# The routed mixtures of layers 0 and 2 run in two halves of eight batches instead of one pass over sixteen

## The chip, the cores and the metric

One core of a Trainium2 chip runs the whole kernel. The metric is device time in microseconds, from one launch, as the median of several executions. One execution was also recorded by the profiler, and all rows below are from it. TensorE is PE in the rows (PEld its weight loads), VectorE is DVE, ScalarE ACT, GpSimd POOL, and SyncE, which only issues DMAs here, SP.

## The reference, cut to what matters

A tower of four layers works on x, 16 batches of 128 tokens of width 128. Each layer adds a gated cross attention and a gated feed-forward part to x. The feed-forward parts of layers 0 and 2 are mixtures of eight experts. The reference lets each token's two best experts count (layer 2 shown):

```python
    logits = jnp.einsum('btd,de->bte', x, Wg) + bg
    top2_vals, top2_idx = jax.lax.top_k(logits, 2)
    scores = jax.nn.softmax(top2_vals, axis=-1)
    onehot = jax.nn.one_hot(top2_idx, E, dtype=x.dtype)
    combine = jnp.einsum('btk,btke->bte', scores, onehot)
    h = jnp.einsum('btd,edh->bteh', x, W1) + b1[None, None]
    h = jax.nn.gelu(h, approximate=False)
    y = jnp.einsum('bteh,ehd->bted', h, W2) + b2[None, None]
    out = jnp.einsum('bted,bte->btd', y, combine)
    return _layer_norm(x + out, gamma, beta)
```

Layer 0 has two first matrices (silu of one times the other), a threshold in place of the product as such, and no outer normalisation. Layer 1's feed-forward part is a chain of four dense matrices (Mlp in the kernel), layer 3's a third mixture that isn't routed by lists.

## The kernel before, in words

The program is a row of phases: Attn0, Routed0, Mlp, Attn2, Routed2, Attn3, Experts3. Each engine has its own instruction list, written out by hand. At the end of a phase, `end_phase` (L163) lets four engines drain and all wait for each other.

**Router, beside the attention.** Batches are taken in four groups of four. While the attention runs, `Router` (L1023) finishes what it can for each group, in phases of one attention step: statistics and normalised x (XNB, stored to the tensor xn in memory), its turn, logits, first and second maximum (`dve_first`, `dve_second`), sums over tokens, ranks (`ranked`), places, and lists. A list says which token stands at which row of which expert. It is made on TensorE by a product of two one-hot sets, AT (128x128, VectorE) and BT (128x128, POOL), eight each. Group g can start only when its four batches leave the attention. So the last groups' phases remain when the attention is over: `tail` (L1174) runs six more steps (TAIL = 6) on every engine with nothing beside them. In it also come `pe_tiles` and `pe_tokens` (L1153, L1164), which turn counts and lists into the table: the expert of each tile, its tokens (IDX) and first rows.

**Tiles.** 4096 pairs of token and expert fill tiles of 128 rows, each of one expert. Each expert may end in a part-filled tile, so 32 + 7 = 39 tiles are run, whatever the routing (NT, L1630). `Routed` is a software pipeline over them: POOL gathers a tile's rows of x (XG, L1696, three tiles ahead) and makes ONE (L1705), a one-hot set that picks the expert's bias row; TensorE turns XG (L1727); ScalarE and VectorE split the result in two parts, XH and XL (L1734, L1739); TensorE makes the products with three pairs of parts and the bias (L1756 to L1759). In step i TensorE does the turn of tile i+1, the first products of i, the turn of the hidden values of i-1 and the second product of i-2 (`pe`, L1761). In layer 0 ScalarE makes SG, VectorE TT (L1910) and, behind the turn, ST (L1924); in layer 2 ScalarE makes SG and SH, VectorE SL (L1988). Y is then taken out by VectorE and stored by SP to the tensor ys. The weights of a tile are chosen by a register with the expert's number, read from the table.

The turned hidden values alternate between two PSUM banks in layer 0 (`pe_units`, L1912). Its second weights W2 are cast in this phase: two of four 1024-column pieces are loaded by SP at its start to a buffer of their own.

**Sums.** For each batch POOL gathers two rows of ys per token (GA, L2197), and VectorE adds both with their weights (L2204, L2207). This is done in the next phase: in Mlp (L2405, L2466) batches 0 to 3 come before anything else, the others between; in Attn3 (`dve_sum`, L2740) batch by batch. ys is written until the end of the tiles, so no gather can begin earlier.

## Time and profile before

| | |
|---|---|
| median of 3 runs | 1191.19 us (1189.45 to 1194.58) |
| the profiled execution | 1195.1 us, its span 1193.8 us |
| TensorE busy, share of span | 907.6 us, 76% |
| VectorE busy | 663.1 us, 56% |
| POOL busy | 474.8 us, 40% |
| ScalarE busy | 396.4 us, 33% |
| mean granted clock of TensorE | 0.833 |
| chain that ended last | TensorE 57%, VectorE 19%, issue 8%, POOL 7%, DMA 5% |

The busy times say how long an engine worked, not whether something waited for it. The stages differ: some are one full engine, others a chain of short steps over many engines. The granted clock is the share of full speed at which TensorE was allowed to run; 1.0 is 2.4 GHz and 0.5 is 1.2 GHz. The kernel is read by stages, and a stage by its timeline.

### The profile page before, as it was taken

Reading aid. Unit: us, or ns where it says so; the run is one execution under the profiler, and the core shown is the slowest. Engines: PE = TensorE matmul, PEld = TensorE weight load, DVE = VectorE, ACT = ScalarE, POOL = GpSimd, SP = SyncE. Lnnn points to the kernel's source line nnn. Section 1 sums busy time; section 2 is a strip of 40 time slices with the busy share of each in tenths; the row PEclk is TensorE's granted clock in tenths of the full one; section 3 lists DMA queues with packets and bytes.
Section 4 is the critical chain, followed back from the end, with each engine's and each line's share of the span. In section 5 each row is a group of like instructions: output and inputs, shape, how many; then the busy total and the mean of one; then the engine's idle time right before and its main releaser. Section 6 shows DMA issues by size and latency. Waiting matters only on the chain.

```text
span 1193.8 us, 22685 instructions
## 1 busy us (share of the span) xinstructions
PE 907.6 (76%) x8131; PEld 723.2 (61%) x8131; DVE 663.1 (56%) x1792; ACT 396.4 (33%) x737; POOL 474.8 (40%) x786
## 2 busy tenths in 40 slices
PE   3776675299992698896777763899658888888898
PEld 2455464278881577675566553799536666777555
DVE  3677663566664655542356544455565676641565
ACT  0343341032221232331244320455402445543412
POOL 5443433444434455225455444555273444200100
PEclk9988665589996699998699855899855999986999
DMA  5211111111123100001122200221211000000262
GB/s 180 82 48 54 33 32 45 66 30 45 45 39 94 47 18 14 5 1 43 54 55 64 59 10 9 56 54 51 47 43 43 26 23 26 16 8 10 63 203 89
DMA packets 48843, 57.59 MB, mean 48 GB/s; under 512 B 7008, under 2 KB 34688, under 8 KB 48352
## 3 DMA queue, kind: packets, MB, share of 16 engines
q1 hardware_dynamic: 43760, 45.65, 12.7%
q0 software_dynamic: 4544, 9.32, 3.3%
q8 instruction: 70, 1.15, 0.4%
q10 hardware_dynamic: 432, 1.18, 0.2%
q14 instruction: 37, 0.30, 0.1%
HBM read 42.02 MB, written 8.32 MB: 42 GB/s over the span
## 4 chain that ended last, share of the span: by engine, by line
PE 57%; DVE 19%; issue 8%; POOL 7%; DMA 5%; ACT 3%; SPq 1%; POOLq 0%; DVEq 0%; ACTq 0%
PE banks L412 9%; DVE NM L482 6%; PE banks L420 4%; PE bank L181 4%; PE bank L433 3%; PE banks L175 3%; PE banks L177 3%; PE banks L176 3%; PE banks L1756 3%; PE bank L2108 2%; POOL BT L1377 2%; PE banks L1759 2%; PE banks L1758 2%; PE banks L1757 2%; PE bank L1999 2%
## 5 line engine op out<-in xcount | busy, mean ns | idle before, releaser
L412 PE MATMUL banks<-KT,QT 31*128 31x128 f32 (+1 forms) x1280 | 165.1, 395 | 95.6 <-DVE NM L482 49.0
L482 DVE TENSOR_REDUCE NM<-banks 128x4 f32<-128x1024 f32 (+1 forms) x112 | 136.6, 1219 | 127.6 <-PE banks L412 127.4
L412 PEld LDWEIGHTS banks<-KT,QT 31*128 31x128 f32 x1280 | 116.4, 230 | 129.5 <-DVE NM L482 56.7
L456 ACT ACTIVATE EE<-banks 128x1024 f32<-128x1024 f32 x112 | 114.7, 1024 | 202.0 <-PE banks L420 201.9
L420 PE MATMUL banks<-QT,KT 32*128 32x128 f32 x1792 | 164.3, 329 | 3.5 <-ACT EE L456 2.5
L420 PEld LDWEIGHTS banks<-QT,KT 32*128 32x128 f32 x1792 | 136.1, 225 | 8.6 <-issue 7.5
L1696 POOL DMA_INDIRECT XG<-xn,SL x78 | 80.2, 1028 | 21.6 <-issue 12.8
L2197 POOL DMA_INDIRECT GA<-ys,PI x64 | 68.1, 1064 | 40.9 <-DMA ys<-Y 25.3
L433 PE MATMUL bank<-EE,VV 128*32 128x128 f32 x1792 | 78.0, 325 | 0.8 <-ACT EE L456 0.8
L1705 POOL TENSOR_SCALAR ONE<-CP,EC 128x128 fp32r<-128x128 f32 x78 | 30.4, 389 | 95.2 <-PE bank L1938 54.9
L433 PEld LDWEIGHTS bank<-EE,VV 128*32 128x32 f32 x1792 | 56.2, 129 | 13.3 <-issue 9.2
L175 PE MATMUL banks<-HH,W1H 128*128 128x512 f32 x128 | 52.5, 411 | 8.2 <-DVE HH L2464 8.1
L1734 ACT CAST XH<-bank 128x128 fp32r<-128x128 f32 x78 | 20.7, 266 | 109.7 <-PE bank L1727 109.7
L1377 POOL TENSOR_SCALAR BT<-CP,PR 128x128 fp32r<-128x128 f32 x64 | 45.9, 733 | 19.1 <-DVE PR L1279 19.1
L177 PE MATMUL banks<-HH,W1L 128*128 128x512 f32 x128 | 51.3, 401 | 0.0
L1988 DVE TENSOR_TENSOR SUL<-bank,SUH 128x512 fp32r<-128x512 f32 x39 | 27.0, 692 | 43.3 <-ACT SUH L1983 43.3
L176 PE MATMUL banks<-HH,W1H 128*128 128x512 f32 x128 | 51.0, 398 | 0.0
L2464 DVE TENSOR_TENSOR HH<-GG,HH 128x512 fp32r<-128x512 f32 x32 | 23.3, 739 | 46.8 <-POOL HH L2485 46.8
L1924 DVE TENSOR_SCALAR ST<-bank 128x512 fp32r<-128x512 f32 x39 | 27.0, 691 | 38.7 <-PE bank L181 38.7
L1759 PE MATMUL banks<-BI,ONE 128*128 128x512 f32 x117 | 47.2, 403 | 0.0
L1999 PE MATMUL bank<-W,SUH 128*128 x156 | 41.3, 342 | 1.4 <-DVE Y L1827 1.4
L2370 ACT ACTIVATE GG<-banks,VC 128x512 f32<-128x512 f32 x32 | 21.6, 687 | 49.5 <-PE banks L177 47.4
(369 smaller groups left out, 2331.3 us busy)
## 6 DMA issues: line engine op xcount, KB each, us to landing
RAW<-in_w SPq DMA_DIRECT2D x20, 512.0 KB, 3.8
CBS<-cw SPq DMA_DIRECT2D x32, 256.0 KB, 3.6
ys<-Y SPq DMA_DIRECT2D x78, 64.0 KB, 1.5
RAW<-in_w SPq DMA_DIRECT2D x8, 352.0 KB, 3.3
KT<-in_keys SPq DMA_DIRECT2D x8, 256.0 KB, 3.1
KT<-KQ SPq DMA_DIRECT2D x32, 64.0 KB, 1.9
QT<-KQ SPq DMA_DIRECT2D x32, 64.0 KB, 1.9
CTX<-in_ctx SPq DMA_DIRECT2D x3, 512.0 KB, 6.8
```

The source lines that it names most:

```text
L175: pe.matmul(out, ah, bh, start=start, stop=False)
L176: pe.matmul(out, ah, bl, start=False, stop=False)
L177: return pe.matmul(out, al, bh, start=False, stop=stop)
L412: ins = pe.matmul(out, self.QT[r, b1 % 4, 128 * g:128 * g + 128], moving(r, 128 * g), start=True, stop=True)
L420: ins = pe.matmul(K.SB[:, 512 * i + 128 * m:512 * i + 128 * m + 128], keys(kb, r, 128 * g), self.QT[r, b3 % 4, 128 * g:128 * g + 128], sta ...
L433: ins = pe.matmul(self.K.PS[4][32 * u:32 * u + 32, 128 * g:128 * g + 128], self.VV[:, slots[kb], 32 * h:32 * h + 32], self.weights(b, h, k ...
L456: act.activation(self.EE[:, b % 2, 2 * p:2 * p + 2, :].rearrange("p i k -> p (i k)"), self.K.SB[:, :], ACT.Exp).then_inc(sig("ee").sem, 1)
L482: dve.tensor_reduce(out, src, AX.X, ALU.max, negate=True).then_inc(sig("m1").sem, 1)
L1377: ins = pool.tensor_scalar(self.BT[:, 4 * j + i, :], K.cp("iota"), self.RO[:, j, 4 * g + i:4 * g + i + 1], 1.0, ALU.is_equal, ALU.mult)
L1696: pool.indirect_dma_start(self.XG[:, t % 4, :], None, self.R.xn, bass.IndirectOffsetOnAxis(ap=self.IDX[:, t:t + 1], axis=0)).then_inc(sig( ...
L1759: return pe.matmul(bank, one, self.BI[:, bias:bias + n], start=False, stop=True)
L2197: pool.indirect_dma_start(self.GA[:, b % 8, j, :], None, K.ys, bass.IndirectOffsetOnAxis(ap=K.PI[:, j, b:b + 1], axis=0)).then_inc(sig(f"g ...
```

## The change

Both mixtures (layers 0 and 2) are split into half 0 (batches 0 to 7) and half 1 (batches 8 to 15), each with its own list, table, xn and ys.

- A half has 16 + 7 = 23 tiles, so 46 are run and not 39. The tail steps and `pe_tiles`, `pe_tokens` are gone. The table of half 0 is made in the last step of the attention (`pe_table(0)`, `dve_table(0)`).
- What remains of groups 2 and 3 stands in the tile loops: TensorE at steps 1, 3, 5, 7, 10, 14 and 16, VectorE at 2, 3, 4, 6, 7, 8, 10, 11, 12, 13, 15 and 17 (the table of half 1), POOL at 4, 5, 8, 13 and 14, ScalarE at 0 and 4. The positions are made in two parts, at 20 and 40.
- The sums of batches 0 to 7 are gathered by POOL at every second tile from 29 and added by VectorE from step 32, to X (layer 0) or DEP (layer 2). Their buffer is that of the raw biases. Mlp and Attn3 sum only batches 8 to 15.
- BT has 64 columns. ONE is made by ScalarE, ahead of XH of the same tile. The hidden values of layer 0 are turned to one bank only (the other is the router's). W2's third piece is loaded over the raw biases once these are split, the fourth by the ring of weight buffers. The bias product of Y has 128 columns. Names and ring numbers follow.

```diff
             self.early.sp(s)
-        self.early.tail(self.LAST, self.early.sp)
...
-    def __init__(self, K, st, router):
+
+    HALF = Router.TILES
+    NT = 2 * Router.TILES
...
-        K.ys = self.ys = K.nc.dram_tensor(f"ys{tag}", (self.NT * 128, 128), F32, kind="Internal").ap()
+        self.sums = Sums(K, self.BRAW[:, 0:1024].rearrange("p (b j d) -> p b j d", b=4, j=2), 0, 8, target)
+        K.ys = self.ys = [K.nc.dram_tensor(f"ys{tag}{h}", (self.HALF * 128, 128), F32, kind="Internal").ap() for h in range(2)]
...
+        R.sp_normal(3)
...
-    def pool_one(self, t):
-        K, pool, sig = self.K, self.K.nc.gpsimd, self.K.sig
-        if t == 0:
-            pool.wait_ge(*sig("t_one")(1))
-        if t >= 4:
-            pool.wait_ge(*sig("second")(t - 3))
-        pool.tensor_scalar(self.ONE[:, t % 4, :], K.cp("ones"), self.EC[:, t:t + 1], 1.0, ALU.mult,
-                           ALU.mult).then_inc(sig("one").sem, 1)
...
             self.pool_gather(t)
         for t in range(self.NT):
-            self.pool_one(t)
             if t + 3 < self.NT:
                 self.pool_gather(t + 3)
             self.pool_more(t)
+            self.pool_router(t)
+            b = t - self.HALF - 6
+            if b >= 0 and b % 2 == 0 and b // 2 < 8:
+                if b == 0:
+                    K, sig = self.K, self.K.sig
+                    K.nc.gpsimd.wait_ge(*sig("y_pos")(1))
+                    K.results = [self.stored(n) for n in range(self.HALF - 3, self.HALF)]
+                self.sums.pool(b // 2)
         self.K.results = [self.stored(t) for t in range(self.NT - 3, self.NT)]
+
+    def pool_router(self, t):
+        R = self.R
+        if t in (4, 5):
+            R.pool_rows(2, t - 4)
+        if t == 8:
+            R.pool_power(3)
+        if t in (13, 14):
+            R.pool_rows(3, t - 13)
...
+            read = self.pe_router(i, read)
+
+    def pe_router(self, i, read):
+        R = self.R
+        if i == 1:
+            read = R.pe_rank(2, read)
+        if i == 3:
+            read = R.pe_turn(3, read)
+        if i == 5:
+            read = R.pe_logits(3, read)
+        if i == 7:
+            read = R.pe_list(2, read)
+        if i == 10:
+            read = R.pe_rank(3, read)
+        if i == 14:
+            read = R.pe_list(3, read)
+        if i == 16:
+            read = R.pe_table(1, read)
+        return read
...
         self.act_more(0, 4)
+        self.act_one(0)
         self.act_hi(0)
         for i in range(self.NT + 2):
             if 0 <= i - 2:
                 self.act_units(i - 2)
             if i + 1 < self.NT:
+                self.act_one(i + 1)
                 self.act_hi(i + 1)
             if i < self.NT:
                 self.act_first(i)
             if i == 0:
                 self.act_more(4, 8)
+                self.R.act_normal(3)
+            if i == 4:
+                self.R.act_turned(3)
+
+    def act_one(self, t):
+
+        K, act, sig = self.K, self.K.nc.scalar, self.K.sig
+        h, k = self.of_table(t)
+        if k == 0:
+            act.wait_ge(*sig("table")(h + 1))
+        if t >= 4:
+            act.wait_ge(*sig("second")(t - 3))
+        act.activation(self.ONE[:, t % 4, :], K.cp("ones"), ACT.Copy, scale=self.EC[:, h, k:k + 1]).then_inc(sig("one").sem, 1)
...
         self.dve_bias()
-        self.dve_more(0, 4)
         self.dve_lo(0)
+        self.dve_more(0, 2)
...
+            if i == 0:
+                self.dve_more(2, 4)
             if i == 1:
                 self.dve_more(4, 6)
-                self.dve_positions()
+            self.dve_router(i)
+            if i == 20:
+                self.dve_positions(0)
+            if i == 40:
+                self.dve_positions(1)
+            b = i - self.HALF - 9
+            if b >= 0 and b % 2 == 0 and b // 2 < 8:
+                self.sums.dve(b // 2)
+
+    def dve_router(self, i):
+        R = self.R
+        if i == 2:
+            R.dve_places(2)
+        if i in (3, 4):
+            R.dve_columns(2, i - 3)
+        if i == 6:
+            R.dve_first(3, *R.logits(3)[0:3])
+        if i == 7:
+            R.dve_second(3, *R.logits(3))
+        if i == 8:
+            R.dve_list(2)
+            R.dve_sums(3)
+        if i == 10:
+            R.dve_weights(3)
+        if i == 11:
+            R.dve_places(3)
+        if i in (12, 13):
+            R.dve_columns(3, i - 12)
+        if i == 15:
+            R.dve_list(3)
+        if i == 17:
+            R.dve_table(1)
...
-        for n in range(2, 4):
-            self.K.nc.sync.dma_start(self.RAW2[:, 2 * n - 4:2 * n - 2, :],
-                                     self.K.A["w0"][:, 2 * n:2 * n + 2, 1024:1536]).then_inc(self.K.sig(f"w2_in{n}").sem, 16)
+
+        K, sig = self.K, self.K.sig
+        K.nc.sync.wait_ge(*sig("bi")(1))
+        K.nc.sync.dma_start(self.BRAW[:, 0:1024].rearrange("p (e k) -> p e k", e=2),
+                            K.A["w0"][:, 4:6, 1024:1536]).then_inc(sig("w2_in").sem, 16)
+        K.sp_raw(self.raw2 + 2, K.A["w0"][:, 6:8, 1024:1536], 1024)
...
-        if t >= 2:
-            pe.wait_ge(*sig("st")(t - 1))
-        K.turn4(pe, K.PS[4 + t % 2], self.TT[:, t % 2, :]).then_inc(sig("t_turned").sem, 1)
+        if t >= 1:
+            pe.wait_ge(*sig("st")(t))
+        K.turn4(pe, K.PS[4], self.TT[:, t % 2, :]).then_inc(sig("t_turned").sem, 1)
...
-        pe.matmul(y, self.ONE[:, t % 4, :], self.BI[:, 1024:1280], start=False, stop=True).then_inc(sig("second").sem, 1)
+        pe.matmul(y[:, 0:128], self.ONE[:, t % 4, :], self.BI[:, 1024:1152], start=False, stop=True).then_inc(sig("second").sem, 1)
...
-            pool.indirect_dma_start(self.GA[:, b % 8, j, :], None, K.ys,
-                                    bass.IndirectOffsetOnAxis(ap=K.PI[:, j, b:b + 1], axis=0)).then_inc(sig(f"ga{b % 4}").sem, 16)
+            pool.indirect_dma_start(self.GA[:, k % self.homes, j, :], None, K.ys[b // 8],
+                                    bass.IndirectOffsetOnAxis(ap=K.PI[:, j, b:b + 1], axis=0)).then_inc(sig(f"ga{k % 4}").sem, 16)
...
         self.dve_w1(0, 4)
-        for b in range(4):
-            self.sums.dve(b)
         self.dve_stats1(0)
...
-                        self.sums.dve(4 * f + 2 * k)
-                        self.sums.dve(4 * f + 2 * k + 1)
+                        if f >= 2:
+                            self.sums.dve(4 * f + 2 * k)
+                            self.sums.dve(4 * f + 2 * k + 1)
...
-            if s + 4 < NBAT:
+            if 8 <= s + 4 < NBAT:
                 self.sums.pool(s + 4)
```

Left out are `pe_table`, `dve_table` and the router's functions, which are the old code cut into one function per piece, with half the width where a list or table is meant.

TensorE, from the tail of the attention of layer 0 to the first tile. OS, OC and OREP are sums and counts, SL and LIS table and list, TV and VB which tiles exist, XTR the turned x. Before:

```order
L181 MATMUL bank<-CP,XNB 128x128 x4
L1146 MATMUL bank<-AT,BT 128x128 x8
L1123 MATMUL bank<-WS,XTR 128x8 x4
L1133 MATMUL bank<-OC,CP 128x32
L1134 MATMUL bank<-OS,CP 128x32
L1158 MATMUL bank<-CP,OREP 128x1
L1160 MATMUL bank<-TV,CP 128x1
L1162 MATMUL bank<-SL,CP 128x40
L1146 MATMUL bank<-AT,BT 128x128 x8
L1169 MATMUL bank<-CP,VB 128x8
L1172 MATMUL bank<-SL,LIS 128x40
L1727 MATMUL bank<-CP,XG 128x128 x2
```

With the change (L1182 to L1184 are the table of half 0, L1789 the turn of a tile's rows):

```order
L1138 MATMUL bank<-WS,XTR 128x8 x4
L374 MATMUL bank<-CP,OT 128x128 x4
L433 MATMUL bank<-EE,VV 32x128 x16
L1182 MATMUL bank<-SL,CP 128x23
L1183 MATMUL bank<-SL,LIS 128x23
L1184 MATMUL bank<-CP,TV 128x8
L374 MATMUL bank<-CP,OT 128x128 x4
L1789 MATMUL bank<-CP,XG 128x128 x2
```

The eleven router rows before stand behind the last output of the attention (L374), with TensorE doing nothing else; now three products, the table, stand ahead of that output, and the others between tiles.

VectorE, one step of the tile loop of layer 0, before:

```order
L1924 TENSOR_SCALAR ST<-bank 128x512
L1825 COPY Y<-bank 128x128
L1827 TENSOR_TENSOR Y<-bank,Y 128x128
L1910 TENSOR_TENSOR TT<-banks,SG 128x512
L1739 TENSOR_TENSOR XL<-bank,XH 128x128
```

And the end of step 6 of the change (L2045 is TT, L1801 XL, L1231 to L1243 the logits and first maximum of group 3):

```order
L2045 TENSOR_TENSOR TT<-banks,SG 128x512
L1801 TENSOR_TENSOR XL<-bank,XH 128x128
L1231 TENSOR_TENSOR LGR<-bank,BR 128x32
L1235 TENSOR_SCALAR LGR<-LGR 128x32
L1236 TENSOR_REDUCE RMR<-LGR 128x4
L1237 TENSOR_TENSOR KKR<-LGR,RMR 128x32
L1238 TENSOR_TENSOR KKR<-KKR,DSR 128x32
L1239 TENSOR_REDUCE RMR<-KKR 128x4
L1240 TENSOR_TENSOR OA<-KKR,RMR 128x32
L1241 SCALAR_TENSOR_TENSOR LGR<-OA,LGR 128x32
L1242 TENSOR_REDUCE RMR<-LGR 128x4
L1243 TENSOR_TENSOR RMR<-RMR 128x4
```

Ten router operations stand between XL of one step and ST of the next. Other steps have four to ten such operations or none.

POOL, in the first half of layer 0's tiles, before:

```order
L1876 TENSOR_TENSOR W<-RAW,W 128x4x128 x2
L1705 TENSOR_SCALAR ONE<-CP,EC 128x128
L1696 DMA XG<-xn,SL 128x128
L1705 TENSOR_SCALAR ONE<-CP,EC 128x128
L1696 DMA XG<-xn,SL 128x128
```

And with the change, from tile 14 into the second half (BRAW is the buffer of the sums there):

```order
L1751 DMA XG<-xn,SL 128x128 x15
L2332 DMA BRAW<-ys,PI 128x128 x2
L1751 DMA XG<-xn,SL 128x128 x2
L2332 DMA BRAW<-ys,PI 128x128 x2
L1751 DMA XG<-xn,SL 128x128 x2
```

ONE is gone from POOL, and two gathers from ys stand behind every second gather of a tile.

## Rows read from the trace of the kernel before

**Rows 1.** Table of stages: stretch, length, busy (instructions) of each engine, clock, DMA.

```profile
core 0: us, PE busy (x) PEld busy (x) DVE busy (x) ACT busy (x) POOL busy (x), PEclk, DMA share, GB/s
196.00:228.70 32.70, 11.50 (x46) 10.27 (x46) 16.78 (x89) 2.23 (x5) 14.13 (x21) 0.52 0.14 41
...
252.20:358.30 106.10, 106.09 (x630) 91.76 (x631) 68.63 (x174) 30.04 (x70) 44.98 (x67) 1.00 0.18 43
...
440.00:460.00 20.00, 14.78 (x65) 10.77 (x64) 12.56 (x31) 6.72 (x9) 8.56 (x12) 1.00 0.04 10
```

**Rows 2.** Timeline, layer 0, from the last X to the experts: start, us, what.

```profile
195.39 0.35 DVE L746 SCALAR_TENSOR_TENSOR X<-ON,TG,X 128x128 f32<-128x128 f32 x1
...
199.19 0.21 DVE L1258 SCALAR_TENSOR_TENSOR WGT<-RMR,TG 128x4 f32<-128x4 f32 x1
...
228.72 0.34 SPq L1660 DMA_DIRECT2D BRAW<-in_bias  x1
```

**Rows 3.** Timeline, layer 0, bias and first products of tiles 3 and 38.

```profile
233.93 1.53 DVE L1686 TENSOR_TENSOR BI<-BRAW,BI 32x1280 fp32r<-32x1280 f32 x1
...
252.21 0.49 PE L1756 MATMUL banks<-W13H,XH 128*128 x1 [0.27 <-issue]
...
358.29 0.40 PE L1756 MATMUL banks<-W13H,XH 128*128 x1
```

**Rows 4.** Timeline, layer 2, the same places as in 2 and 3.

```profile
712.45 0.35 DVE L2508 SCALAR_TENSOR_TENSOR X<-bank,TG,X 128x128 f32<-128x128 f32 x1 [0.21 <-PE bank L2624]
...
745.68 0.34 SPq L1660 DMA_DIRECT2D BRAW<-in_bias  x1
...
759.53 0.50 PE L1756 MATMUL banks<-W12H,XH 128*128 x1
...
849.18 0.40 PE L1756 MATMUL banks<-W12H,XH 128*128 x1
```

**Rows 5.** Timeline, layer 0, one tile in the middle.

```profile
304.45 0.68 DVE L1910 TENSOR_TENSOR TT<-banks,SG 128x512 f32<-128x512 f32 x1
...
305.67 0.60 PE L181 MATMUL bank<-CP,TT 128*128 128x128 f32 x4
...
306.31 0.69 DVE L1924 TENSOR_SCALAR ST<-bank 128x512 fp32r<-128x512 f32 x1 [0.98 <-PE bank L181]
```

**Rows 6.** Timeline, layer 2, one tile in the middle.

```profile
803.32 0.37 POOL L1705 TENSOR_SCALAR ONE<-CP,EC 128x128 fp32r<-128x128 f32 x1 [1.01 <-PE bank L2002]
803.37 0.27 ACT L1734 CAST XH<-bank 128x128 fp32r<-128x128 f32 x1 [0.51 <-PE bank L1727]
...
804.02 0.28 DVE L1739 TENSOR_TENSOR XL<-bank,XH 128x128 fp32r<-128x128 f32 x1
```

**Rows 7.** Timeline, layer 0, router of group 3: logits, first and last of ten operations.

```profile
209.95 1.88 PE L1123 MATMUL bank<-WS,XTR 128*128 128x8 f32 x8 [0.38 <-DVE LIS L1304]
211.87 0.19 DVE L1217 TENSOR_TENSOR LGR<-bank,BR 128x32 f32<-128x32 f32 x1 [1.97 <-PE bank L1123]
...
213.87 0.16 DVE L1229 TENSOR_TENSOR RMR<-RMR 128x4 f32<-128x4 f32 x1
```

**Rows 8.** Page, costliest groups: busy us, mean ns, idle before.

```profile
L2197 POOL DMA_INDIRECT GA<-ys,PI x64 | 68.1, 1064 | 40.9 <-DMA ys<-Y 25.3
```

**Rows 9.** Timeline, Mlp: a cast of W1, the first turn, the wait for HH.

```profile
377.06 0.87 ACT L2349 CAST W1H<-RAW 128x352 fp32r<-128x352 f32 x2 [0.84 <-DMA RAW<-in_w]
...
385.94 0.87 PE L181 MATMUL bank<-CP,XB 128*128 128x128 f32 x3 [19.86 <-DVE XB L246]
...
411.59 0.50 PE L175 MATMUL banks<-HH,W1H 128*128 128x512 f32 x1 [2.16 <-DVE HH L2464]
```

**Rows 10.** Timeline, Attn3: QT filled, the step behind sum 0, TensorE's first work.

```profile
859.36 1.22 DVE L290 TENSOR_SCALAR QT<-CP 128x2048 f32<-128x2048 f32 x1
...
864.34 0.28 DVE L2744 TENSOR_TENSOR X<-X,GB 128x128 f32<-128x128 f32 x1
...
871.47 0.45 PE L2839 MATMUL bank<-CP,XN 128*128 128x128 f32 x1 [15.30 <-POOL XN L258]
```

More of the change, by code:

```diff
@@ L1136, in pe @@
[L1136 to L1138 removed]
+            freed = self.pe_rank(g, freed)
         g = self.phase(s, 6)
         if g is not None:
[L1141 to L1146 removed]
@@ L3005, in first_two @@
         with ExitStack() as st:
-            router.beside(st)
             P = Attn0(K, st, router)
```

504 lines of the change are left out of this document (263 added, 241 removed).

## The prediction

> **What bounds the kernel now.** I read the table of stages first. In layer 0's tiles TensorE works 106.09 of 106.10 us at granted clock 1.00, the upper of its two levels (2.4 GHz), and the 32.7 us ahead of them hold 11.50 us of TensorE at 0.52 [rows 1]. The kernel thus has two kinds of stretch: full ones, where only TensorE's own work counts, and lead-ins, which are chains of small steps. The change shortens lead-ins and lengthens full stretches.
>
> Then the timeline of layer 0's lead-in: the last X of the attention ends at 195.74; the weights of group 2 end at 199.40; the experts' first DMA is issued at 228.72 [rows 2]. Between stand router steps of groups 2 and 3. The first products of tiles 3 and 38 begin at 252.21 and 358.29, so a tile costs 106.08/35 = 3.03 us [rows 3]. In layer 2 the last X begins at 712.45, the first DMA at 745.68, and tiles 3 and 38 at 759.53 and 849.18: 2.56 us a tile [rows 4].
>
> Last, the slack of the other engines in a tile. Layer 0: TT ends at 305.13 and TensorE's turn of it begins at 305.67, 0.54 us of slack; VectorE is idle 0.98 us ahead of ST [rows 5]. Layer 2: XH ends at 803.64, and XL, which reads it, begins at 804.02, 0.38 later [rows 6].
>
> **The change, part by part.** Times are against the profiled execution (1195.1 us, span 1193.8), which lies 3.9 over the median of the three runs (1191.2).
>
> (a) The six tail steps go. After the last X there are left the statistics of group 3, the second maximum, sums and weights of group 2 (to 199.40), and the new table of half 0: four small VectorE operations of 0.22 each (the pitch in [rows 7]), 0.9. So the attention ends near 200.3 and not 228.7: **-28.4**. Layer 2 keeps the same list; its last X ends at 712.8 [rows 4], plus the same 4.55 is 717.3, against 745.68: **-28.4**. The barrier stays.
>
> (b) Tiles 0 to 3 of layer 0. Before, tile 3 comes 23.5 after the first DMA; in layer 2, which has no second weights to fetch in this stage, 13.9 [rows 2, 3, 4]. Now the gather has the queues to itself (W2's loads wait for bi, which ended at 235.46, 6.7 in [rows 3]), tile 0 starts earlier, but ScalarE must then wait for W2, cast four pieces, and normalise group 3 before XH of tile 2. Bounds 0 and -9.6; nearer to the first since W2 is now issued later: **-3.5**. In layer 2 the rank of group 2 (4 passes) goes among cold tiles: 4 x 0.235 = **+0.9**, the pass from the logits' row, 1.88 us for 8 at the lower level (1.2 GHz) [rows 7].
>
> (c) Seven tiles more in each: 7 x 3.03 = **+21.2**, and 7 x 2.56 = **+17.9**, the pitches of [rows 3, 4]. The bias product loses 128 of its 256 columns; the weight load beside it stays, so nothing is gained.
>
> (d) Router work on TensorE beside tiles. Passes: logits 8, list of group 2 8, rank with its count 6, list of group 3 with its rank 10, table 6, that is 38 at half of 0.235 at the upper level, 4.5 us, and a turn of four, some 0.4 of its row's 0.60 [rows 5]: **+4.8** in each layer, **+9.6**. It is added in full, since TensorE has no idle time there. Behind each piece the next tile's turn waits, and ScalarE and VectorE get that much slack.
>
> (e) Router work on VectorE. The ten operations of the first maximum go from 211.87 to 214.03, 2.16 us, 0.22 each [rows 7]; two sets of places are ten too, positions nine wider ones, and the other pieces four to six, so 0.9 to 1.3 each: some 20 us a layer. What is longer than idle plus slack (0.98 + 0.54 [rows 5], taken for layer 2 too) holds TensorE up. Tiles 2, 6, 11 have 2.16 (0.6 too much each), 20 and 40 have the positions, 1.9 (0.35 each): 0.6 x 3 + 0.7 = **+2.5** a layer, **+5**. Bounds: 0, if TensorE's own pieces give the time back, and the whole, 20 a layer. The idle time [rows 5] is nearer to the first.
>
> (f) ONE goes from POOL (0.37) to ScalarE, ahead of XH; the nearest ScalarE row is XH, 0.27. Either fits in the 0.38 of room [rows 6]: **0**. If nothing of it fitted, 46 + 46 = 92 tiles of 0.37 make 34. The single bank for the turned tile: ST ends at 307.00, and the next turn, one pitch behind 305.67, writes it at 308.70 [rows 5]: 0, with 1.7 to spare.
>
> (g) Sums of batches 0 to 7. POOL issues four gathers in two tiles, at 1.06 [rows 8] 4.3 of layer 2's 5.1 us, a fit with little over: 0. VectorE's two operations fit in its idle time. In the next stage what stood in the way is gone. Mlp: TensorE's first turn was at 385.94. What is late next is W1's seventh piece, whose cast begins at 377.06: 0.43 of cast, 0.5 of VectorE for its low part and 1.3 of normalising put the turn at 379.3 [rows 9]: **-6.6**. The four sums in group 0's first two steps go too; they stand ahead of the third HH, for which TensorE idled 2.16 [rows 9]: **-2.2**. Attn3: the step behind sum 0 began at 864.34 and TensorE at 871.47; now VectorE is free for it when QT is filled, 860.6 [rows 10]. 3.8 is the one bound; the other is 6.3, if the 7.1 between, in which batch 1's gather and sum stand, shrink to their other operations, some 4.6. Four gathers ahead of it on POOL go too, so nearer to the second: **-6**.
>
> (h) BT has 64 columns for 128. That is POOL's time, for which the attention's lists of groups 0 and 1 do not visibly wait: 0.
>
> Sum: -28.4 - 28.4 - 3.5 + 0.9 + 21.2 + 17.9 + 9.6 + 5 - 6.6 - 2.2 - 6 = -20.5. That is 1195.1 - 20.5 = 1174.6 as a profiled execution, and 1191.2 - 20.5, **1171**, in the measure of the median.
>
> **The rivals.** *Router pieces hold the tiles up by their whole length* (0.15). VectorE would pass on 20 us a layer for 2.5: +35, 1206; half of it, 1188. For: each piece stands between two parts of a tile, in order. Against: the 0.98 of idle time in each 3.03 [rows 5].
>
> *ONE on ScalarE lengthens every tile* (0.06). Place: XH of tile i+1 waits behind ONE, and XL behind XH. Price 0.37 x 92 = 34 at most: 1205, slower. From 20.5/92 = 0.22 us a tile it eats the whole gain, from 0.29 the kernel is slower by over 0.5%. Against: the 0.38 of room.
>
> *The clock falls in the tiles with router work* (0.04). TensorE's holes of 0.6 us would make its clock drop, and cold tiles cost twice: 16 tiles a layer, 16 x (3.03 + 2.56) = +89, 1260; a quarter of that, 1193. Against: Mlp's stretch from 440 to 460 has TensorE busy only 14.78 of 20 us and clock 1.00 [rows 1]. The Trainium skill, TensorE: Matmul & The Clock Gate, section HAM oscillation — how this bites in real kernels, says that a TensorE that keeps pausing between groups of matmuls falls back to the lower clock again and again. By that rule the result would be nearer to 1260; the row on Mlp speaks for a clock that stays.
>
> *The sums and lead-ins give more* (0.12): VectorE's pieces hidden whole (-5), Attn3's first steps with fewer VectorE and POOL operations (-3), ScalarE quicker at tile 2 (-4): 1159.
>
> *The second half is not ready* (0.03): the table of half 1 comes late, tile 23 waits, and the tail is back in another place, 1190. It is made at tile 17, six tiles or 15 us ahead, and the gathers begin three ahead; so hardly.
>
> **Numbers.** My forecast, 1163 to 1179, has 0.60. With the better case and the milder half of the first rival the range is 1157 to 1188. A measurement can tell about 0.5%, 6 us, from no change. Faster by more than that: 0.60 + 0.12 + 0.05 of the first rival, 0.77. Within: 0.07 of the first rival, 0.03, and 0.03 of the clock's and ONE's, 0.13. Slower: 0.03 of the first rival and 0.07 of ONE's and the clock's, 0.10.
>
> **What would show it.** Right: first product of layer 0 near 208 and tile 3 near 220; 46 tiles at 3.03 and 2.56 but for tiles 2 to 17, which take some 7 us more together in each layer; no idle TensorE behind XH; Mlp's first turn 12 us behind its first load's issue, and no VectorE wait for a gather in either stage's start. Wrong: a pitch over 3.2 in tiles 24 and on (ONE or gathers), a granted clock under 0.95 in tiles 3 to 17, or an attention that still ends 10 us behind its last X.

## The result, and the profile after

The changed kernel takes 1161.4 us (median of 4 runs, 1156.9 to 1164.2) against 1190.3 for the kernel before (4 runs, 1188.1 to 1194.6): a ratio of 0.974, 95% interval 0.971 to 0.977. I had forecast 1171, with a range of 1157 to 1188. That is inside the range, but 1.6 under the 1163 to 1179 to which the forecast gave its 0.60, and nearest to the case in which sums and lead-ins give more (1159, with 0.12). The gain is 29 us in the medians and 34 between the two profiled runs (1195.1 and 1161.3); the sum said 20.5.

First the table of stages of the kernel after, to be held against [rows 1]. Columns as there.

```profile
core 0: us, PE busy (x) PEld busy (x) DVE busy (x) ACT busy (x) POOL busy (x), PEclk, DMA share, GB/s
199.20:203.60 4.40, 0.00 (x0) 0.00 (x0) 3.94 (x26) 0.00 (x0) 1.62 (x4) 0.50 0.00 0
251.90:355.40 103.50, 102.19 (x612) 87.17 (x612) 75.46 (x215) 38.06 (x98) 47.59 (x54) 1.00 0.23 51
```

The lead-in of 32.7 us with 11.5 us of TensorE in it has become one of 4.4 us with none. The full stretch (34 tiles of layer 0, from 12 to 45) is still full, 102.19 of 103.50 us at clock 1.00. Then the timeline at the places of [rows 2 to 4]: the last X of the first attention, the first load of the experts, the first product of tile 3 in layer 0, Mlp's first load and its first turn; after that the same for layer 2, and Attn3's first load and first TensorE work.

```profile
199.12 0.35 DVE L743 SCALAR_TENSOR_TENSOR X<-ON,TG,X 128x128 f32<-128x128 f32 x1
...
203.60 0.34 SPq L1711 DMA_DIRECT2D BRAW<-in_bias  x1
...
225.50 0.48 PE L1819 MATMUL banks<-W13H,XH 128*128 x1
...
367.32 0.85 SPq L189 DMA_DIRECT2D RAW<-in_w  x2
...
378.64 1.09 PE L181 MATMUL bank<-CP,XB 128*128 128x128 f32 x4 [12.42 <-DVE XB L246]
...
700.58 0.35 DVE L2637 SCALAR_TENSOR_TENSOR X<-bank,TG,X 128x128 f32<-128x128 f32 x1 [1.16 <-PE bank L2752]
...
704.94 0.35 SPq L1711 DMA_DIRECT2D BRAW<-in_bias  x1
...
843.19 0.54 SPq L2906 DMA_DIRECT2D KT<-in_keys  x1
...
849.08 0.45 PE L2965 MATMUL bank<-CP,XN 128*128 128x128 f32 x1 [9.33 <-POOL XN L258]
```

From last X to first load there are now 4.48 us in layer 0 and 4.36 in layer 2, before 33.33 and 33.23 [rows 2, 4]. Tile 3 begins 21.90 behind the load, before 23.49 [rows 2, 3]. Mlp's first turn is 11.32 behind its first load, Attn3's first TensorE work 5.89 behind its own. In the kernel before the two loads, and a turn in Attn3 that comes up under (g), were these:

```profile
367.19 0.37 SPq L189 DMA_DIRECT2D RAW<-in_w  x1
...
859.52 0.54 SPq L2780 DMA_DIRECT2D KT<-in_keys  x1
...
878.14 0.48 PE L2839 MATMUL bank<-CP,XN 128*128 128x128 f32 x1 [4.22 <-DVE VV L2953]
```

Cut at such loads, the two executions differ by stage as follows (us; a tile stage reaches from the experts' first load to the next stage's first load):

| stage | before | after | difference |
|---|---|---|---|
| start to last X of the first attention | 195.39 | 199.12 | +3.7 |
| last X to the experts' load, layer 0 | 33.33 | 4.48 | -28.9 |
| tile stage, layer 0 | 138.47 | 163.72 | +25.3 |
| Mlp | 185.93 | 175.56 | -10.4 |
| second attention, to its last X | 159.33 | 157.70 | -1.6 |
| last X to the experts' load, layer 2 | 33.23 | 4.36 | -28.9 |
| tile stage, layer 2 | 113.84 | 138.24 | +24.4 |
| Attn3, to X of batch 10 | 193.61 | 184.43 | -9.2 |
| Attn3, batch 10 to last X | 47.79 | 40.16 | -7.6 |
| last experts | 92.86 | 92.02 | -0.8 |

Two stages that the change does not touch moved by +3.7 and -7.6. Whether that is the change or the execution, what the sums beside the tiles cost, and which of the small terms were real was for the runs to say.

### The profile page after: what moved, and what is told of

Its sections match the earlier page's. It is cut to its first block, busy times and chain, and to the rows that moved or that the text cites. A ratio compares the mean times of both kernels' runs of the same rounds, so it can differ in the third digit from the quotient of the medians.

```text
span 1159.8 us, 23669 instructions
## 1 busy us (share of the span) xinstructions
PE 938.8 (81%) x8403; PEld 747.1 (64%) x8403; DVE 685.2 (59%) x1883; ACT 439.8 (38%) x864; POOL 438.7 (38%) x726
## 4 chain that ended last, share of the span: by engine, by line
PE 61%; DVE 19%; issue 6%; DMA 6%; ACT 4%; POOL 3%; SPq 1%; DVEq 0%; POOLq 0%; ACTq 0%
PE banks L412 10%; DVE NM L482 7%; PE bank L181 4%; PE banks L420 4%; PE banks L175 3%; PE banks L1819 3%; PE banks L177 3%; PE banks L176 3%; PE bank L433 3%; PE banks L1820 3%; PE banks L1822 3%; PE banks L1821 3%; PE bank L2134 2%; PE bank L2243 2%; PE bank L2071 2%
## 5 line engine op out<-in xcount | busy, mean ns | idle before, releaser
L412 PE MATMUL banks<-KT,QT 31*128 31x128 f32 (+1 forms) x1280 | 169.8, 404 | 89.7 <-DVE NM L482 44.7
L456 ACT ACTIVATE EE<-banks 128x1024 f32<-128x1024 f32 x112 | 114.7, 1024 | 193.6 <-PE banks L420 193.6
L1751 POOL DMA_INDIRECT XG<-xn,SL x92 | 89.7, 975 | 101.5 <-PE bank L1789 88.6
L1890 ACT ACTIVATE ONE<-CP,EC 128x128 fp32r<-128x128 f32 x92 | 37.0, 403 | 78.7 <-PE bank L2073 54.8
L1822 PE MATMUL banks<-BI,ONE 128*128 128x512 f32 x138 | 55.5, 402 | 0.0
L2123 DVE TENSOR_TENSOR SUL<-bank,SUH 128x512 fp32r<-128x512 f32 x46 | 31.7, 690 | 34.4 <-ACT SUH L2118 34.2
L2134 PE MATMUL bank<-W,SUH 128*128 x184 | 48.6, 341 | 2.0 <-DVE Y L1958 1.9
L2059 DVE TENSOR_SCALAR ST<-bank 128x512 fp32r<-128x512 f32 x46 | 31.7, 690 | 30.9 <-PE bank L181 30.7
L1789 PE MATMUL bank<-CP,XG 128*128 128x128 f32 x92 | 28.4, 308 | 21.8 <-DMA XG<-xn,SL 18.4
L1819 PE MATMUL banks<-W13H,XH 128*128 x92 | 41.1, 447 | 2.4 <-issue 2.3
L2135 PE MATMUL bank<-W,SUL 128*128 x184 | 40.9, 222 | 0.0
```

The lines of the kernel that those rows point to most:

```text
L412: ins = pe.matmul(out, self.QT[r, b1 % 4, 128 * g:128 * g + 128], moving(r, 128 * g), start=True, stop=True)
L456: act.activation(self.EE[:, b % 2, 2 * p:2 * p + 2, :].rearrange("p i k -> p (i k)"), self.K.SB[:, :], ACT.Exp).then_inc(sig("ee").sem, 1)
L1751: pool.indirect_dma_start(self.XG[:, t % 4, :], None, self.R.xn[h], bass.IndirectOffsetOnAxis(ap=self.IDX[:, h, k:k + 1], axis=0)).then_in ...
L1819: pe.matmul(bank, xh, wh, start=True, stop=False)
L1822: return pe.matmul(bank, one, self.BI[:, bias:bias + n], start=False, stop=True)
L2134: pe.matmul(y, self.SH[:, t % 2, c], w, start=(k == 0), stop=False)
```

## The experiments

There were twelve runs, in three batches of four; a late update, as explained under e1, is what sets the batches apart. The record gives the first batch chip number 15 and the second and third both number 9, and it is the first and the third that behave alike. So what differs goes with the batch; that it belongs to a chip, as the expectations below take it, is not shown. The kernel before was timed in each batch: 1201.6, 1192.0 and 1197.2 us (11, 11 and 15 runs). Ratios are to those of the same batch.

### e1, e2: the two kernels once more (first batch)

No edit. Of e1, the kernel after, was expected:

> The changed kernel once more. Theory A (the change itself gave 28 to 29 us; the 34 between the two profiled runs hold some 5 us of clock that differ from execution to execution): time 1157 to 1165 us, and in the new profile the first attention (to its last X) and the end of the third attention (first 40.15 us at granted clock 0.92, before 47.8 at 0.72) come out at other lengths than in the first profile, by 2 us or more. Theory B (a shorter end of the third attention is a fixed effect of the change): its end again near 40 us at a granted clock near 0.92, and the first attention again near 199.

Of e2, the kernel before:

> The kernel before once more, one look. Theory A (clock differs by execution): the end of the third attention, from the first X of batch 10 to the last X, is not again 47.8 us at clock 0.72 but lies between 40 and 48. Theory B (a fixed property of this kernel): 47 to 48.5 us again, and the whole at 1188 to 1195.

Measured: e1 1183.5 us (6 runs, 1178.9 to 1191.2), ratio 0.9875 (0.983 to 0.992); e2 1202.4. The same kernel that had gained 2.6% gained 1.25% here, which neither theory had. The first attention took 192.2 and the end of Attn3 43.5 at clock 0.80, so in the kernel after those two do change from execution to execution. In the kernel before they did not: e2 has 195.6 and, for the end of Attn3, 47.79 us again, the length of its theory B (whose 1188 to 1195 for the whole it missed). But the tile stages took 166.8 and 148.0 us, where the first profile had 163.7 and 138.2, and that is no matter of the clock. Here is the stretch in layer 2 from tile 32's turn to tile 42's, with sums beside the tiles, in the table of stages, first of the kernel after in its first profile, then of e1.

```profile
795.81:821.52 25.71, 25.71 (x182) 23.07 (x182) 17.23 (x54) 16.31 (x40) 19.18 (x21) 1.00 0.34 79
```

```profile
797.61:828.05 30.44, 27.44 (x182) 23.09 (x182) 18.74 (x56) 16.17 (x40) 19.68 (x21) 1.00 0.29 66
```

Ten tiles in 25.71 us, TensorE never idle; and the same 182 instructions at the same clock 1.00 in 30.44 us, with 3.0 us idle. What ended that idle time is in the groups of costliest instructions (line, count, busy us, mean ns, idle us before them and what ended it), in layer 2's second product, first of the kernel after:

```profile
L2134 PE MATMUL bank<-W,SUH 128*128 x184 | 48.6, 341 | 2.0 <-DVE Y L1958 1.9
```

and of e1:

```profile
L2134 PE MATMUL bank<-W,SUH 128*128 x184 | 49.3, 345 | 7.7 <-DVE Y L1958 7.6
```

TensorE waits for VectorE's Y, 7.6 us against 1.9. One step further back is a report that comes late. Kernel after, first profile, where the sums begin: two gathers of ys, the end of a product, and ScalarE's SG, which by the program waits for that product (and an older turn) alone:

```profile
787.44 0.95 POOL L2332 DMA_INDIRECT BRAW<-ys,PI  x1 [0.30 <-issue]
...
788.69 0.94 POOL L2332 DMA_INDIRECT BRAW<-ys,PI  x1 [0.30 <-issue]
...
789.03 0.39 PE L1822 MATMUL banks<-BI,ONE 128*128 128x512 f32 x1
...
789.46 0.60 ACT L2101 ACTIVATE SG<-banks 128x512 f32<-128x512 f32 x1 [0.60 <-PE banks L1822]
```

The same place in e1:

```profile
787.25 0.95 POOL L2332 DMA_INDIRECT BRAW<-ys,PI  x1 [0.30 <-issue]
...
788.50 0.95 POOL L2332 DMA_INDIRECT BRAW<-ys,PI  x1 [0.30 <-issue]
...
788.87 0.39 PE L1822 MATMUL banks<-BI,ONE 128*128 128x512 f32 x1
...
789.76 0.95 POOL L1751 DMA_INDIRECT XG<-xn,SL  x1 [0.30 <-issue]
...
790.94 0.60 ACT L2101 ACTIVATE SG<-banks 128x512 f32<-128x512 f32 x1 [1.90 <-DMA xn<-XNB]
```

The product ends at 789.42 and SG begins 0.04 later; in e1 it ends at 789.26 and SG begins 1.68 later. (The profile names a DMA as the releaser, "xn<-XNB"; SG waits for no DMA.) The trace's semaphore events say the same: in e1 the product's update is noted at 790.92. I call an update late that comes over 0.2 us behind the end of its instruction. There are 81 in e1 and 25 in e2, none in the first profile of the kernel before and 1 in that of the kernel after (such counts are good to a few). TensorE's stand beside gathers that follow each other closely: the two of a sum in Attn3 (in the kernel before too, where e2 took 200.5 us to batch 10 and not 193.6), and the rows of three or four where sums lie beside tiles, 29 in e1's tile stages. In the ten tiles above, each of the five pairs of tiles has a turn of hidden values whose update is 0.9 to 1.1 us late, and a pair takes 6.1 us for 5.1: the 4.7 us are these five delays.

### e3: the sums back in the next stages (first batch)

```diff
 # Routed.pool and Routed.dve
-                self.sums.pool(b // 2)
-                self.sums.dve(b // 2)
 # Mlp, Attn3: all 16 again, in the places of the kernel before
-        self.sums = Sums(K, K.sb(st, "GA0", [128, 8, 2, 128]), 8, 8, lambda b: K.X[:, b, :])
+        self.sums = Sums(K, K.sb(st, "GA0", [128, 8, 2, 128]), 0, 16, lambda b: K.X[:, b, :])
```

> The changed kernel with all 16 sums of each layer made in the next stages, as in the kernel before. Theory A (sums stood in the way of both starts): the first turn of the MLP stage comes 18.5 us behind its first load again and not 11.3, third attention's first TensorE work at 12 and not 5.9, in all 9 to 10 us in the MLP stage and 8 to 9 us in the attention, less 1 us that tiles 40 to 45 get back: 1161.4 + 17 = 1178 us. Theory B (the starts are shorter for another reason, such as a shorter queue of transfers in front): less than 6 us longer, under 1168 us.

Measured: 1183.6 us (6 runs), ratio 0.9856 (0.981 to 0.991), no different from e1. Theory A's stages came: Mlp 185.8 (e1: 175.5) and Attn3 to batch 10 197.0 (e1: 189.9). But the tile stages gave it back: 162.8 and 137.5, 4.0 and 10.5 less than e1, with one late update of TensorE in the two where e1 has 29. In this batch the sums beside the tiles cost what they saved behind them. So theory A's total, 17 us over the kernel after, did not come: the medians are equal.

### e4: ONE on GpSimd (first batch)

```diff
 # Routed.act
-                self.act_one(i + 1)
 # Routed.pool, ahead of the gather, as tensor_scalar
+            self.act_one(t)
```

> The changed kernel with the mask ONE of each tile made on GpSimd ahead of the gather, as before, and no longer on ScalarE. Theory A (ONE's 0.40 us on ScalarE fits beside TensorE): no difference outside of the first four tiles, pitch 3.04 and 2.56 in tiles 24 to 38, 1161 within 2 us; at the start of layer 0 tile 3 comes some 0.4 us earlier. Theory B (ScalarE's ONE costs time): up to 0.4 us a tile, down to 1143 us. Theory C (GpSimd is full with gathers, sums and router rows): tiles 32 to 45 get longer than 3.1 us and the kernel is slower than 1165.

Measured: 1177.2 us (6 runs), ratio 0.9818 (0.977 to 0.987); the interval overlaps e1's, and the tile stages are 168.7 and 145.4 (e1: 166.8 and 148.0), so neither place is shown to be faster. In the tiles with room the place of ONE makes no difference: from tile 17's turn to tile 30's in layer 0 it is 40.63 us here and 40.62 in e1. ONE itself is 403 ns on ScalarE and 406 on GpSimd. At the start theory A was wrong, tile 4's turn came 23.5 us behind the load and not 19.8. In the tiles with sums GpSimd is full, as theory C has it, but e1 is slow there too: from tile 31's turn to tile 42's in layer 2 it is 34.9 us, in e1 33.3, though e1 loses more at tiles 31 and 43. Theory B, up to 18 us to be had from ScalarE, is out: nothing is gained where nothing else is in the way.

### e5 to e7: the measure, gathers spread, start and positions (second batch)

e5 is the kernel after, unchanged.

> The changed kernel a third time, as the measure for the three runs beside it. Theory A (late reports: in the first repetition TensorE's reports of finished work reached the others up to 2 us late while three or four indirect gathers went out in a row, and tiles 31 to 43 of layer 2 took 3.05 us each and not 2.57; it depends on the chip that the run falls on): either a chip as in the first profile, with 1157 to 1165 us, layer 2's tile stage at 138 us and no late reports, or one as in the repetition, with 1178 to 1191 us and 145 to 149 us for that stage. Theory B (noise of one execution): a stage of 138 to 141 us in this profile whatever the total.

e6 puts a sum's two gathers beside two tiles:

```diff
-            if b >= 0 and b % 2 == 0 and b // 2 < 8:
+            if 0 <= b < 16:
-                self.sums.pool(b // 2)
+                self.sums.pool(b // 2, (b % 2,))
-            b = i - self.HALF - 9
+            b = i - self.HALF - 10
```

> The changed kernel with the two gathers of each sum in the tile stages put into two different steps, one a tile, so that at most two gathers follow each other and not four, and the sum one step later. Theory A (late reports come of the row of gathers): where e5 shows a tile stage of 145 to 149 us in layer 2 and 166 or more in layer 0, this one shows under 141 and under 165, 8 to 12 us less in the whole; where e5 shows no late reports, no difference (within 2 us). Theory B (any gather of ys beside a tile delays, in a row or not): the same stages as e5 within 2 us.

e7 is e6 with two edits more:

```diff
             if i == 0:
-                self.act_more(4, 8)
+                self.act_more(4, 6)
+            if i == 1:
+                self.act_more(6, 8)
                 self.R.act_normal(3)
-            if i == 40:
+            if i == 26:
                 self.dve_positions(1)
```

> The kernel of e6 with two edits more: the last two casts of W2 and the normalising of group 3 one step later on ScalarE (tile 2's XH no longer behind them), and the table positions of the second half at step 26, away from the sums. Theory A (term (b): ScalarE's casts hold up tile 2): tile 4 of layer 0 comes 2 to 4 us earlier behind the first load than the 21.9 of the first profile, and the end of the tile stages is 0.5 to 1 us shorter in each layer, 3 to 6 us less than e6 in all. Theory B (the start waits for the weights' arrival and not for ScalarE's order): tile 4 at the same place within 1 us, and no difference in the whole beyond 1.5 us.

Measured: e5 1158.2 us (6 runs, 1151.5 to 1161.3), ratio 0.972 (0.969 to 0.975); e6 1159.9, 0.974 (0.970 to 0.978); e7 1151.9 (1148.6 to 1163.5), 0.967 (0.962 to 0.972). e5 repeats the first result: no late TensorE update, tile stages 162.1 and 138.2. So e6 had nothing to mend. In e7's profile tile 4's turn comes 18.3 us behind the load (first profile 21.9, e6 19.6), as theory A has it; layer 0's tile stage is 159.8, 1.2 under e6 and 2.2 under e5; layer 2's is 138.2, no gain (e6: 137.4): there tile 5 takes 3.71 us (e6: 2.93), presumably behind the normalising at step 1. (A tile's time is here and below from the turn before it to its own turn.) The interval of e7 overlaps e5's, so the 6 us between their medians are not shown to be real.

e5 also bears on the two stages that moved. The end of Attn3, batch 10 to last X, with its granted clock: of the kernel before,

```profile
1053.00:1101.00 48.00, 41.59 (x549) 34.54 (x549) 13.85 (x36) 19.73 (x31) 1.62 (x4) 0.72 0.01 2
```

of the kernel after in its first profile,

```profile
1027.60:1067.80 40.20, 32.75 (x549) 26.94 (x549) 13.69 (x35) 19.73 (x31) 1.62 (x4) 0.92 0.01 3
```

and of the same kernel after in e9 of the third batch.

```profile
1045.77:1094.59 48.82, 42.56 (x549) 35.13 (x549) 13.65 (x35) 19.85 (x31) 1.62 (x4) 0.69 0.01 2
```

The same 549 instructions in 48.0 us at 0.72, 40.2 at 0.92, 48.8 at 0.69; in e5 38.7 at 0.96. Four profiles of one kernel cover the whole range, so the -7.6 of the first pair needs no part of the change to explain it. That the change has no part in it is not shown: both profiles of the kernel before have 47.8, the four of the kernel after 38.7 to 48.8. Nor is the +3.7 at the start: the kernel after took 192.2, 193.3 and 193.7 there in its other profiles, less than the kernel before (195.4, 195.6).

### e8: blocks of extra work (second batch)

The kernel of e3 with work that nothing uses. Its computation is otherwise whole.

```diff
 # Routed.dve: small VectorE operations, each waiting for the last
+            for n in range({24: 5, 26: 10, 29: 15, 32: 20}.get(i, 0)):
+                self.R.dve_small(self.tax(n))
 # Routed.pe: matmuls of the logits' form
+            for n in range({36: 8, 38: 16}.get(i, 0)):
+                pe.matmul(self.R.T[:, 0:8], self.R.XT[:, 0:128], K.wt(self.R.wname)[:, 0:8], start=True, stop=True)
```

> The kernel of e3 (sums in the next stages, so the tiles from 24 on are free of extras) with extra work without use put beside single tiles: 5, 10, 15 and 20 small VectorE operations (0.22 us each: 1.1, 2.2, 3.2, 4.3 us) at steps 24, 26, 29 and 32, and 8 and 16 passes of TensorE of the logits' form at steps 36 and 38. By the prediction's rule (what is longer than 0.98 of idle time and 0.54 of slack holds TensorE up) the VectorE blocks lengthen the tiles around them by 0, 0.6, 1.7 and 2.8 us; by the rival, their whole length: 1.1, 2.2, 3.2, 4.3; by what the changed kernel's first profile suggests (VectorE's pieces of ten cost nothing): 0, 0, 0.9 or less, 2 or less. TensorE's passes: 0.94 and 1.9 us by the prediction's price, half of that if they are hidden behind other work.

Timeline of e8, layer 0, the turns of tiles 31 to 36, with the block of 20 and TensorE's wait behind it:

```profile
304.33 0.29 PE L1781 MATMUL bank<-CP,XG 128*128 128x128 f32 x1
...
308.81 0.28 PE L1781 MATMUL bank<-CP,XG 128*128 128x128 f32 x1
...
312.25 0.28 PE L1781 MATMUL bank<-CP,XG 128*128 128x128 f32 x1
...
313.83 3.90 DVE L1917 TENSOR_TENSOR RMR<-RMR 128x4 f32<-128x4 f32 x20
...
315.21 0.29 PE L1781 MATMUL bank<-CP,XG 128*128 128x128 f32 x1
...
319.64 0.66 PE L181 MATMUL bank<-CP,TT 128*128 128x128 f32 x4 [2.14 <-DVE TT L2043]
...
320.67 0.28 PE L1781 MATMUL bank<-CP,XG 128*128 128x128 f32 x1
...
324.13 0.28 PE L1781 MATMUL bank<-CP,XG 128*128 128x128 f32 x1
```

Each turn is one tile; a block shows two to four turns later. The operations took 0.195 us each. Against the same three turns of e3 the blocks cost:

| block, us | by the rule (less 1.52) | layer 0 | layer 2 |
|---|---|---|---|
| 5 operations, 1.0 | 0 | 0.0 | -0.1 |
| 10, 1.95 | 0.4 | 0.8 | 0.6 |
| 15, 2.9 | 1.4 | 1.5 | 1.8 |
| 20, 3.9 | 2.4 | 2.9 | 4.0 |

The rule, idle time plus slack, is right within 0.4 us up to 15 operations beside a plain tile; a long block in layer 2 comes at its full length. The expectation drawn from the first profile (0, 0, 0.9, 2) was too low, and the rival's whole length too high but for that block. For TensorE I had miscounted my own edit: a matmul of the logits is recorded as two passes, so the blocks are 16 and 32 passes. The first:

```profile
330.13 1.90 PE L1840 MATMUL bank<-WS,XTR 128*128 128x8 f32 x16
...
331.88 0.31 PE L1781 MATMUL bank<-CP,XG 128*128 128x128 f32 x1
```

Its tile took 4.80 us for 3.05, 1.75 more, or 0.11 a pass (forecast: 0.1175); 32 passes cost 3.5. TensorE's price was right and is paid in full. The tile behind the 32 lost 1.3 and 1.4 more; the reason stays open.

### e9 to e12: the same four questions once more (third batch)

The edits are none (e9), that of e6 (e10), of e7 (e11) and of e3 (e12).

> The changed kernel a fourth time, as the measure for the three runs beside it. If the chip is as in the first profile and e5 (no late reports): 1155 to 1164 us; if it is as in the first repetition: 1178 to 1191 us, with layer 2's tile stage at 145 us or more.

> The kernel of e6 again (one gather of a sum in each tile, not two in every second). e5 had no late reports, so e6 could not tell. Theory A (late reports come of the row of gathers): on a chip with them 8 to 12 us under e9, tile stages under 141 and 165 us; on one without them within 3 us of e9. Theory B (any gather of ys delays): within 3 us of e9 on either.

> The kernel of e7 again. e7's median was 6 us under e5's, yet its profile shows 2.2 us less in layer 0's tile stage and none in layer 2's. Theory A (the edits are worth what the profile shows): 2 to 3 us under e9. Theory B (the 6 us are real, by something that the one profile did not show): 5 us or more under e9. Theory C (scatter of the clock): within 1 us of e9 or over it.

> The kernel of e3 again (all sums in the next stages). On the chip of e3 it was as fast as the changed kernel, 1183.6 against 1183.5, since the gathers beside the tiles cost there what they saved in the stages behind. Theory A (on a chip without late reports the sums beside the tiles are nearly free): 16 to 20 us slower than e9: 10.4 in the MLP stage, 9 to 11 in the third attention, 0 to 2 given back in the tile stages. Theory B (they cost the tiles on every chip): within 6 us of e9.

| | us (runs) | ratio, interval | tile stage 0 | tile stage 2 | Mlp | Attn3 to batch 10 | late updates |
|---|---|---|---|---|---|---|---|
| e9, after | 1188.1 (6) | 0.989, 0.983 to 0.995 | 167.8 | 151.4 | 175.4 | 190.9 | 82 |
| e10, spread | 1178.7 (6) | 0.987, 0.982 to 0.992 | 164.5 | 148.7 | 176.0 | 192.4 | 82 |
| e11, start too | 1174.9 (6) | 0.984, 0.979 to 0.989 | 161.1 | 152.5 | 175.9 | 190.8 | 75 |
| e12, sums back | 1185.2 (10) | 0.990, 0.986 to 0.994 | 163.2 | 137.6 | 185.7 | 200.3 | 41 |

This batch is of the first batch's sort: late updates in all, the kernel after at 1.1% only. e12 is as fast as e9, so for this sort of batch theory B of the sums holds. It is not a test of theory A, which speaks of the other sort; there e8, with the sums back, gives the stages (Mlp 185.9, Attn3 to batch 10 194.0, against 175.4 and 183.2 in e5). e10's median is 9.4 us under e9's, the total that theory A of the gathers names, but the intervals overlap and the stages speak against it: one gather of ys a tile, and layer 2 still at 148.7, with 38 late updates of TensorE in the two tile stages (e9: 34, e12: none). Layer 0 gained 3.3, in one profile. TensorE's idle time ahead of the second product, layer 2, of e10 and then of e12 (where the line is L2123):

```profile
L2134 PE MATMUL bank<-W,SUH 128*128 x184 | 49.6, 347 | 6.6 <-DVE Y L1958 6.4
```

```profile
L2123 PE MATMUL bank<-W,SUH 128*128 x184 | 48.6, 341 | 1.5 <-DVE Y L1947 1.4
```

6.4 us with the gathers spread, 1.4 without gathers beside the tiles. e11 is 13 us under e9 in the medians, as theory B has it (5 us or more), but here too the intervals overlap. Between the two profiles layer 0's tile stage is 6.7 shorter, where e9 lost 4.9 us over the pitch at tiles 43 and 44 (5.95 and 5.01 us, with positions, sums and late updates together; e11: 2.96 and 3.50); layer 2's is 1.1 longer. e7 and e11, one kernel, have the lowest ratio of their batches, 0.5% under the kernel after in both, with intervals that overlap each time, and are not shown to be better than the kernel after.

## Why the prediction was right, and where its sum was off

The verdict and the main mechanism held: lead-ins shortened, full stretches lengthened, and the time inside the range. Some of it is errors that cancel: layer 0's tile stage was forecast at +25.0 and measured at +25.3, since (b) saved 1.9 less than forecast and a sum cost 0.6 where 0 stood, while (d) and (e) cost 1.0 and 1.4 less. That this stage came out right is luck. Point by point, against the first profile:

**(a) The tails.** -28.4 twice forecast, -28.9 twice measured.

**(b) Tiles 0 to 3 of layer 0.** -3.5 forecast, 23.49 to 21.90 = -1.6 measured. The mechanism was right, ScalarE's casts and group 3's normalising stand ahead of XH of tile 2, and TensorE waited 2.04 us there. But part of the size is the clock. From tile 3's turn to tile 4's, of the kernel after in its first profile and then in e5:

```profile
219.70:225.40 5.70, 4.78 (x18) 3.88 (x18) 4.47 (x15) 1.24 (x4) 4.12 (x6) 0.70 0.29 81
```

```profile
213.38:217.54 4.16, 3.26 (x19) 2.68 (x19) 3.92 (x13) 1.23 (x4) 2.70 (x3) 1.00 0.37 103
```

Granted clock 0.70 in the one and 1.00 in the other; ahead of it TensorE had idled 2.04 us in the one and 0.97 in the other. e1, e5 and e9 have tile 4's turn 19.7 to 19.8 us behind the load and the first profile 21.85. So the term lies between -1.6 and -3.8, by the execution; e3, e10 and e12, which start layer 0 the same way, have tile 3 at 21.4 to 21.7, and the granted clock fell for a stretch there too. The edit in e7 and e11 takes it to 18.3 and 16.7, though tile 5 gives 0.7 to 1.2 of it back.

**(c) and (d) Tiles and TensorE's router work.** Forecast +21.2, +17.9 and twice +4.8, and +0.9 of cold rank. The rank came as forecast: layer 2's tile 4 has its turn 14.50 behind the load for 13.53. From tile 4's turn to tile 22's the first profile has 58.34 us in layer 0 and 50.35 in layer 2; 18 plain tiles at 3.03 and 2.56 are 54.5 and 46.1. The 3.8 and 4.3 over are less than the 4.8 forecast for TensorE's pieces alone, and nothing is left for VectorE's. Tiles 24 to 42 run at 3.04 and 2.57. The price of a pass was confirmed by e8.

**(e) VectorE's router work.** +2.5 a layer forecast; this is the step that failed. Between tiles 4 and 22 the lower bound held, 0, as the sum under (c) and (d) shows: most of VectorE's pieces come right behind one of TensorE's. Timeline of the kernel after, layer 0, the turn of tile 6, the logits, the turns of tiles 7 and 8, and between them the first and last of VectorE's ten:

```profile
231.75 0.29 PE L1789 MATMUL bank<-CP,XG 128*128 128x128 f32 x1
...
234.87 1.01 PE L1138 MATMUL bank<-WS,XTR 128*128 128x8 f32 x8
...
235.73 0.31 PE L1789 MATMUL bank<-CP,XG 128*128 128x128 f32 x1
...
236.58 0.18 DVE L1231 TENSOR_TENSOR LGR<-bank,BR 128x32 f32<-128x32 f32 x1
...
238.57 0.16 DVE L1243 TENSOR_TENSOR RMR<-RMR 128x4 f32<-128x4 f32 x1
...
238.71 0.29 PE L1789 MATMUL bank<-CP,XG 128*128 128x128 f32 x1
```

The tile with the logits takes 3.98 us, the one with the ten operations 2.98. TensorE's 1.01 gives VectorE the room that I had written down as slack and then not counted. Pieces beside none of TensorE's can be seen: where the columns of group 3 stand (steps 12 and 13), layer 2's tiles 14 and 15 take 2.77 and 2.76 us, 0.2 over the pitch each. The positions cost the most: about 0.5 in layer 0 and 0.3 in layer 2 at step 20 (forecast 0.35), and some 0.6 at step 40, where e7 without them has tiles 43 and 44 at 3.08 and 3.04 for 3.72 and 3.59 in e5, the sum beside them included (without sums, e3 has 3.09 and 3.58). In all some 1.1 us in layer 0 and 0.9 in layer 2, for 2.5 forecast.

**(f) ONE and the single bank.** 0 forecast for both. ONE's is 0 by e4, in the tiles with room. The single bank was never tried apart; tiles 24 to 42 at 3.04 for 3.03 before leave it next to nothing.

**(g) Sums.** Beside the tiles 0 was forecast: right in the first profile and e5 for layer 2's tiles 31 to 42 (2.56), but at tile 43, where a sum meets the positions, 0.6 in layer 0 (3.74, e3: 3.09) and 0.8 in layer 2 (3.35, e3: 2.58); and wrong by 4 to 5 us in layer 0 and 10 to 14 in layer 2 in e1 and e9. Mlp: -8.8 forecast, -10.4 measured, of which 7.4 is the first turn (11.32 behind the load for 18.75); the wait ahead of the third HH fell from 2.16 [rows 9] to this:

```profile
401.48 0.50 PE L175 MATMUL banks<-HH,W1H 128*128 128x512 f32 x1 [0.58 <-DVE HH L2599]
```

Attn3: -6 forecast for its start. TensorE's first work came 5.89 behind the load for 11.95 [rows 10], which is -6.1. Mis-sized was what followed: the next wait, for VV, was 4.22 before and is this now.

```profile
852.54 0.47 PE L2965 MATMUL bank<-CP,XN 128*128 128x128 f32 x1 [1.01 <-DVE VV L3079]
```

That is 3.2 more, and -9.2 to batch 10 in all. e8 against e5 gives 10.5 and 10.9 us for the two stages. In Attn3 I had costed the first wait that the sums stood in and not the second. Of the 8.5 us that the sum lacked against the first medians, this term is 4.8 (1.6 in Mlp, 3.2 in Attn3), the two tile stages together 1.5 (51.1 forecast, 49.6 measured) and the tails 1.0; 1.2 us stay without a place.

**The rivals.** Router pieces at their whole length, ONE on ScalarE and a falling clock in the tiles (1.00 there) did not come. The clock in the tiles with router work, of the kernel after, layer 0 from tile 5's turn to tile 22's:

```profile
228.84:283.79 54.95, 54.89 (x347) 47.55 (x345) 44.12 (x145) 20.53 (x52) 21.69 (x27) 1.00 0.19 42
```

It stays at 1.00. The rule of the Trainium skill that I had weighed there (TensorE: Matmul & The Clock Gate, section HAM oscillation — how this bites in real kernels) finds nothing to act on: its case is a TensorE that waits for a transfer behind every group of matmuls, and here TensorE pauses for 0.06 us in 54.95. The better case did, in two of its three parts (VectorE's pieces, Attn3). What I did not name as a rival was the one that takes half the gain away in some batches: in the first and third the sums with their gathers beside the tiles cost 14.5 (e1 less e3) and 18.4 us (e9 less e12), of which only some 1.4 us, at tile 43, is seen in the first profile too. I had written "a fit with little over: 0" for GpSimd, and what failed was not that fit. GpSimd's four gathers in two tiles took the same time in e1 as in the first profile (those of XG 977 and 975 ns); TensorE's reports came late.

**What stays open.** Why updates come late beside rows of gathers in two batches, and not in the other or in the first result, is open; so is whether it is the chip, since the record has the same number for a batch with it and one without. Whether a sum without indirect gathers would escape it was not tried. With XG's gathers alone TensorE's updates in the tile stages were in time but for one (e3, e12), though some 16 of the other engines' were late there; and spreading does not cure it. Since the kernel before has it too (e2), the ratio is 0.974 or 0.972 in batches without late updates, and 0.988 or 0.989 in the others.

## What to carry to other kernels

Cost a lead-in by following it to its second and third wait, since the work that is taken out of its head stood ahead of those too. Price work put beside a full engine by what that engine itself is given at that step: pieces that come in pairs, TensorE's first and VectorE's behind it, can hide the second, while a block beside a plain tile costs what is longer than idle plus slack. And repeat the winner in another batch before you trust a percent, and the kernel before with it: here the same two kernels gave 2.6%, 1.3%, 2.8% and 1.1%.
